# One product over all 64 keys instead of two over 32: window attention's weighted values on eight 64x32 tiles, with the probabilities copied between partition quarters by DMA

## The chip, the cores and the metric

The kernel runs on one core of one Trainium2 chip. The metric is the device time of one execution in microseconds, the median of several runs. The engines are named as in the profile: PE is TensorE (PEld its weight loads), DVE VectorE, ACT ScalarE, POOL GpSimd, and SP the engine that issues most DMAs.

## The reference

Input is x of 32 sequences x 256 tokens x 128 features, float32. Four residual blocks follow each other, each on the layer norm of its input:

```
x = x + window_attention(norm(x))      # block "P": 16 heads of 8, 2 key/value heads, window 32
x = x + butterfly_ffn(norm(x))         # block "F": 128 -> 512 -> gelu -> 128
x = x + linear_attention(norm(x))      # block "L": elu + 1, 16 heads of 8
x = x + butterfly_ffn(norm(x))         # block "G": the same weights as F
```

In the window attention a block of 32 queries looks at 64 keys (its own 32 and 16 on either side), masked to `(u >= t) & (u < t + 32)` for query t and key u. So each query sees exactly 32 of the 64 keys: of the keys u and u + 32 exactly one is allowed. The probabilities are a softmax over them, and the output is `einsum('bhntu,bhnud->bhntd', probs, vb)`.

## The kernel before, in words

The 8,192 tokens are worked on in 16 groups g of 512 tokens (TILES = 4 tiles j of 128 tokens, each with four windows of 32 queries). Each engine runs a list of steps, called a turn, over and over; a step with lag n in turn t works on group t - n, so several groups are in flight, one in each block. The order inside a turn and the lags are written out by hand in a function `turn` for each engine, and again in tables (PRODUCTS, VECTOR, PROBS, ...) from which the counts of the semaphore waits are made. COVERED lists waits of PE that another wait already implies. PE is in order: a product whose input or PSUM bank isn't ready holds all that are behind it. The first turns also carry the products that multiply out the butterfly weights (steps X.*).

The path of window attention for one tile j of a group is:

- `scores` (L491, W.S j): eight products on 64x32 tiles of the array, 512 columns each, write the scores of 64 keys for 16 heads into the two banks of `ps_s`. Their keys lie in `kx`, which `spread_keys` (L328) fills with eight DMAs from `kv_rows` in DRAM once the last scores of the previous group are done (there is one `kx`).
- DVE: `merge_halves` (L1018, W.cp) puts the allowed one of u and u + 32 in place, `row_max`, `subtract_max`, then `scores_transposed` (L1038, W.tr) transposes 32x32 blocks, so that keys lie on partitions.
- ACT: `probs_out` (L810, W.E) takes the exponential of 512 elements per partition into `probs_m`, one of 2 buffers.
- POOL: `probs_parted` (L419, W.um) multiplies the merged probabilities with two 0/1 masks (`keep`): one half for keys u < 32, one for u >= 32, 1,024 elements per partition into `probs_t`, one of 2 buffers.
- PE: `weighted_values` (L508, W.PV) makes 16 products on 32x32 tiles, 256 columns each. They use eight different tiles, twice: for part u = 0 and accumulated for u = 1.
- DVE: `head_outputs` (L1045 to L1052) transposes, and divides by the sum, which comes as a column of ones in the values `vx`.

The values come from `kv_rows` by `spread_values` (L340, eight DMAs for a group) into `vx_t`, and a DVE transpose into `vx`. A float32 product shows as two records in the trace.

Of the kernel before, what the change touches and what calls it, by code (L numbers as in the profile page):

```python
# [9 lines left out]
ALU = mybir.AluOpType  # L10
# [19 lines left out]
PARTS = SPAN // WIN  # L30
STAGES = HID.bit_length() - 1
INNER = P.bit_length() - 1
KVW = DIM + HEADS
FIRST = [("ident", P), ("last_half", WIN), ("keep", PARTS * WIN), ("wq", P), ("wkv", 2 * KV * HD), ("bq", 1), ("bkv", 1), ("inside", TSPAN), ("bo", P)]
# [33 lines left out]
]  # L68
PHI = [
    ("L.k1", 5), ("L.q", 4), ("L.k0", 4),  # L70
]
PROBS = [
    ("W.E3", 3), ("W.E0", 2), ("W.E1", 2), ("W.E2", 2),
]
POOL_STEPS = [
    ("L.rv", 6), ("L.nm", 6), ("L.rstd", 6), ("L.nmr", 6), ("P.rv", 0), ("P.nm", 0),
    ("P.rstd", 0), ("P.nmr", 0), ("F.rv", 4), ("F.nm", 4), ("F.rstd", 4), ("F.nmr", 4),
    ("W.rv", 3), ("W.nm", 3), ("W.rstd", 3), ("W.nmr", 3),
]
NORMED = [  # L80
    ("L.xn", 6), ("P.xn", 0), ("F.xn", 4), ("W.xn", 3),
# [5 lines left out]
    ("W.um2", 3), ("W.um3", 3), ("W.um0", 2), ("W.um1", 2),  # L87
]
TURNS = NG + 7
CHUNKS = {"a": [0, 1], "b": [2, 3]}  # L90
COVERED = {
    ("F.down", "F.up0"), ("F.down", "F.up2"), ("F.down", "F.up3"), ("F.down", "X.d6"), ("F.down", "bank"),
# [4 lines left out]
    ("G.up3", "X.wT"), ("L.k0", "L.xT"), ("L.k1", "L.xT"), ("L.kv", "L.k0"), ("L.kv", "bank"),  # L97
    ("L.oT", "L.out0"), ("L.out0", "L.q"), ("L.out1", "L.kv"), ("L.out1", "L.q"), ("L.out1", "bank"),
    ("L.q", "bank"), ("P.kv", "P.xT"), ("P.q", "P.xT"), ("W.PV0", "bank"), ("W.S1", "P.q"),
# [10 lines left out]
WINDOW = [[0, 1, 2, 3], [1, 0, 3, 2]]  # L110
# [31 lines left out]
def window_and_linear_attention_with_butterfly_ffn(  # L142
    nc, x, first_c, later_c, outer_c, vones_c, w_exp_t, w_con, up_m, down_m, out,
):
    with ExitStack() as ctx:
# [54 lines left out]
        vx = sb("vx", [P, TILES, KV, PARTS, 32])  # L200
# [3 lines left out]
        probs_m = sb("probs_m", [P, 2, KV, HPK, WIN])  # L204
        probs_t = sb("probs_t", [P, 2, PARTS, KV, HPK, WIN])
# [56 lines left out]
        kx_in = Count(sem("kx_in"), [("P.kx", 0)], 16 * HPK)  # L262
        v_in = Count(sem("v_in"), [("P.v", 0)], 16 * 4 * KV)
# [32 lines left out]
        def _(sp):  # L296
# [51 lines left out]
            def turn(t):  # L348
                for g in due(t, 2):
                    spread_keys(g)  # L350
                for g in due(t, 0):
                    load_x(g)
                for g in due(t, 2):
                    spread_values(g)
                for g in due(t, 7):
                    store_y(g)
                for g in due(t, 1):
                    store_keys(g)
# [7 lines left out]
        def _(pool):  # L366
# [58 lines left out]
            def turn(t):  # L425
                for g in due(t, 4):
                    add_bias(g, "W", bffn_s, "W.proj", "F.down")
                for g in due(t, 3):
                    probs_parted(g, 2)
                for g in due(t, 6):  # L430
                    normalise(g, "L")
                if t == 2:
                    ffn_bias()
                for g in due(t, 0):
                    normalise(g, "P")
                for g in due(t, 3):
                    probs_parted(g, 3)
# [6 lines left out]
                for g in due(t, 6):  # L444
                    add_bias(g, "L", bffn_s, "L.proj", "G.down")
                for g in due(t, 1):
                    add_bias(g, "P", bo_s, None, "W.proj")
                for g in due(t, 3):
                    normalise(g, "W")
# [8 lines left out]
        def _(pe):  # L458
# [38 lines left out]
            def weighted_values(g, j):  # L497
# [154 lines left out]
            def turn(t):  # L652
                for g in due(t, 2):
                    scores(g, 3)
                for g in due(t, 6):
                    ffn_up(g, "G", 3)
                for g in due(t, 5):
                    linear_out(g, 1)
                for g in due(t, 6):
                    ffn_up(g, "G", 0)  # L660
                    ffn_up(g, "G", 2)
                for g in due(t, 3):
                    heads_transposed(g)
                for g in due(t, 5):
                    linear_transposed(g)
                if t == 1:
                    up_stage(2, "b")
                for g in due(t, 6):
# [632 lines left out]
```

## Time and profile before

| what | value |
|---|---|
| three runs | 596.56, 597.85, 598.96 us; median 597.85 us |
| the profiled execution | 597.42 us, span 595.6 us |
| busy: PE, POOL, DVE, ACT | 553.9, 446.7, 445.7, 336.7 us |
| granted PE clock, mean | 0.986 |
| instructions | 16,572 |

The span is from the first to the last instruction of the profiled execution; its own time is 1.8 us longer. Busy times are of each engine by itself, and overlap.

### The profile page before, as it was taken

How to read it: one execution, taken by the hardware profiler on the slowest of the kernel's cores; microseconds unless marked ns; L12 is line 12 of the kernel's file. 1: busy time of each engine (PE TensorE's matmuls, PEld its weight loads, DVE VectorE, ACT ScalarE, POOL GpSimd, SP SyncE). 2: the span in 40 equal slices, each digit the busy share in tenths (PEclk: the TensorE clock that was granted, in tenths of full speed). 3: DMA queues.
4: the chain of work that ended last, by engine and by line, in shares of the span. 5: the costliest groups of instructions: out<-in, count | busy, mean ns of one | idle time of the engine just before them, and what ended most of it. 6: DMA issues, size and time to landing. Idle time of an engine off the chain costs nothing.

```text
span 595.6 us, 16572 instructions
## 1 busy us (share of the span) xinstructions
PE 553.9 (93%) x6068; PEld 355.3 (60%) x6068; DVE 445.7 (75%) x1270; ACT 336.7 (57%) x574; POOL 446.7 (75%) x645
## 2 busy tenths in 40 slices
PE   3867698989999999999999999999999999999986
PEld 2533354556756656666666675665666666777663
DVE  5498878898888878787887888787877878654430
ACT  1321355366667666665666566766666666766532
POOL 6064778798979878897979798887887795956530
PEclk9996989999999999999999999999999999999998
DMA  9410201010101020111101010101010100000001
GB/s 316 134 37 15 52 7 46 13 41 16 39 24 46 25 47 20 33 37 29 43 21 43 16 42 26 45 26 43 21 34 20 29 24 2 19 3 19 0 19 35
DMA packets 37904, 22.48 MB, mean 38 GB/s; under 512 B 8384, under 2 KB 35520, under 8 KB 37824
## 3 DMA queue, kind: packets, MB, share of 16 engines
q1 hardware_dynamic: 35376, 17.21, 11.1%
q10 hardware_dynamic: 2448, 4.22, 2.0%
q8 instruction: 48, 0.79, 0.6%
q14 instruction: 32, 0.26, 0.2%
HBM read 15.91 MB, written 5.51 MB: 36 GB/s over the span
## 4 chain that ended last, share of the span: by engine, by line
PE 82%; DVE 7%; issue 3%; POOL 2%; DMA 1%; ACTq 1%; SPq 1%; ACT 1%; DVEq 0%; POOLq 0%
PE ring L523 20%; PE ring L535 18%; PE ps_o L508 10%; PE ps_s L491 9%; PE ring L472 7%; PE ring L546 5%; PE ring L566 4%; PE ring L606 3%; PE ring L555 2%; PE ring L583 2%; PE ring L576 1%; DVE u_t L289 1%; SPq L328 1%; DMA x_P<-in_x 1%; PE ring L595 1%
## 5 line engine op out<-in xcount | busy, mean ns | idle before, releaser
L419 POOL TENSOR_TENSOR probs_t<-probs_m,first 128x1024 f32<-128x1024 f32 x64 | 150.4, 2362 | 34.7 <-ACT probs_m L810 26.3
L792 ACT ACT_TABLE_LOAD x60 | 77.0, 1283 | 10.8 <-issue 9.7
L802 ACT ACTIVATE hid_G<-ring,b 128x512 f32<-128x512 f32 x64 | 44.0, 687 | 62.0 <-PE ring L523 61.2
L491 PE MATMUL ps_s<-kx,q_t 64*32 64x512 f32 x1024 | 71.0, 611 | 6.8 <-DVE merged L1031 4.3
L508 PE MATMUL ps_o<-probs_t,vx 32*32 32x256 f32 x2048 | 72.5, 392 | 3.1 <-DVE vx L1113 2.8
L523 PE MATMUL ring<-xT_G,w1b 128*128 128x512 f32 x128 | 65.7, 619 | 1.7 <-DVE x_F L1003 1.0
L1018 DVE COPY_PREDICATED ps_s<-first,ps_s 128x512 f32<-128x512 uint32 x64 | 43.6, 682 | 28.0 <-PE ps_s L491 27.6
L535 PEld LDWEIGHTS ring<-w,hid_G 128*128 128x128 f32 x512 | 59.5, 192 | 3.5 <-ACT hid_G L802 1.7
L535 PE MATMUL ring<-w,hid_G 128*128 128x128 f32 x512 | 59.9, 275 | 1.8 <-DVE x_L L1003 1.0
L523 PE MATMUL ring<-xT_F,w1b 128*128 128x512 f32 x128 | 59.2, 605 | 0.7 <-ACT xT_F L780 0.7
L535 PE MATMUL ring<-w,hid_F 128*128 128x128 f32 x512 | 59.9, 275 | 0.0
L535 PEld LDWEIGHTS ring<-w,hid_F 128*128 128x128 f32 x512 | 58.6, 192 | 0.8 <-issue 0.8
L802 ACT ACTIVATE hid_F<-ring,b 128x512 f32<-128x512 f32 x64 | 43.9, 687 | 23.3 <-PE ring L523 23.2
L810 ACT ACTIVATE probs_m<-merged_t 128x512 f32<-128x512 f32 x64 | 39.4, 620 | 22.4 <-POOL probs_t L419 17.2
L1045 DVE STREAM_TRANSPOSE ps_o<-ps_o 128x512 f32<-128x512 f32 x64 | 45.5, 711 | 7.6 <-PE ps_o L508 7.3
L508 PEld LDWEIGHTS ps_o<-probs_t,vx 32*32 32x32 f32 x2048 | 31.5, 106 | 29.1 <-DVE mv_W L982 10.6
L1031 DVE TENSOR_TENSOR merged<-ps_s,rowmax 128x512 f32<-128x512 f32 x64 | 44.0, 687 | 2.8
L523 PEld LDWEIGHTS ring<-xT_F,w1b 128*128 128x128 f32 x128 | 23.0, 189 | 36.4 <-issue 34.5
L1038 DVE STREAM_TRANSPOSE merged_t<-merged 128x512 f32<-128x512 f32 x64 | 44.4, 695 | 0.2 <-ACT probs_m L810 0.2
L1025 DVE TENSOR_REDUCE rowmax<-ps_s 128x16 f32<-128x512 f32 x64 | 43.1, 674 | 0.9 <-issue 0.3
L523 PEld LDWEIGHTS ring<-xT_G,w1b 128*128 128x128 f32 x128 | 21.4, 194 | 22.3 <-issue 21.3
L566 PEld LDWEIGHTS ring<-later,xT_L 128*128 128x128 f32 x128 | 23.2, 189 | 14.7 <-issue 12.3
(114 smaller groups left out, 1071.5 us busy)
## 6 DMA issues: line engine op xcount, KB each, us to landing
kx<-kv_rows SPq DMA_DIRECT2D x128, 40.0 KB, 2.2
x_P<-in_x SPq DMA_DIRECT2D x16, 256.0 KB, 3.2
out_x<-x_G SPq DMA_DIRECT2D x16, 256.0 KB, 2.3
vx_t<-kv_rows SPq DMA_DIRECT2D x128, 8.0 KB
up_s<-in_up_m ACTq DMA_DIRECT2D x7, 256.0 KB, 7.0
down_s<-in_down_m ACTq DMA_DIRECT2D x7, 256.0 KB, 6.9
kv_rows<-kv_t SPq DMA_DIRECT2D x16, 80.0 KB, 1.6
later<-in_later_c SPq DMA_DIRECT2D x1, 584.0 KB, 4.1
```

The lines of the kernel that those rows point to most:

```text
L419: nc.gpsimd.tensor_tensor(probs_t[:, j % 2].rearrange("p u k h t -> p u (k h) t"), probs_m[:, j % 2].rearrange("p (a k) h t -> p a (k h) t ...
L491: last = nc.tensor.matmul(ps_s[32 * i:32 * i + 32, a], q_t[half, P * j + 32 * c:P * j + 32 * c + 32], kx[half, :, TSPAN * j + 32 * c:TSPAN ...
L508: last = nc.tensor.matmul(ps_o[32 * c:32 * c + 32, a, 0:HPK * WIN], vx[rows, j, a, u], probs_t[rows, j % 2, u, a], start=(u == 0), stop=(u ...
L523: nc.tensor.matmul(bank(name)[:], w1b[:, P * c:P * (c + 1)], x_t[s][:], start=True, stop=True).then_inc(product.sem, 1)
L535: last = nc.tensor.matmul(bank(name)[:, P * j:P * (j + 1)], hid[s][:, c, P * j:P * (j + 1)], w2[:, c], start=(c == 0), stop=(c == CH - 1))
L566: last = nc.tensor.matmul(bank(name)[:, 2 * P * i:2 * P * (i + 1)], x_t["L"][:, P * j:P * (j + 1)], wl_s[:, P:3 * P], start=True, stop=True)
L792: nc.scalar.activation(unused[:, i:i + 1], half[0:1, 0:1], function)
L802: nc.scalar.activation(hid[s][:, c], bank(name)[:], ACT.Gelu, bias=b1[:, c:c + 1]).then_inc(drained[BANK[name]].sem, 1)
L1018: nc.vector.copy_predicated(merged_s, last_half.bitcast(mybir.dt.uint32).rearrange("p (a t) -> p a t", a=1) .to_broadcast([P, HEADS, WIN]) ...
L1031: nc.vector.tensor_tensor(merged[:, j % 2].rearrange("p k h t -> p (k h) t"), halves()[0], m, ALU.subtract).then_inc(drained["S"].sem, 1)
L1038: nc.vector.transpose(merged_t[:, j % 2].rearrange("p k h t -> p (k h t)"), merged[:, j % 2].rearrange("p k h t -> p (k h t)")).then_inc(v ...
L1045: nc.vector.transpose(ps_o[:, :, 0:HPK * WIN], ps_o[:, :, 0:HPK * WIN]).then_inc(vec.sem, 1)
```

## The change

Weighted values become eight products for a tile, each over 64 partitions (all 64 keys of a window at once) instead of sixteen over 32. For this the keys u < 32 of a window and those u >= 32 must lie on neighbouring 32-partition quarters, and both quarters need the probabilities:

- ACT writes the exponential twice (1,024 elements per partition in one instruction, its input read twice), straight into `probs_t`, which has a buffer for each of the four tiles now; `probs_m` goes.
- `spread_probs`, new on SP: for each tile, four DMAs of 32 partitions x 2 KB copy each quarter's block into the neighbouring quarter, from `probs_t` to `probs_t`.
- POOL masks in place: 1,024 elements per partition, with one mask whose content depends on the quarter. It waits for the DMAs.
- `spread_values` takes other offsets, and WINDOW, which says which window lies in which quarter, changes for the second key/value head.
- The order of the turn and the lags of every engine are written anew, with the banks of the products, the waits that COVERED leaves out, and TURNS = NG + 9 for NG + 7.

```diff
+PAIR = 2
-        vx = sb("vx", [P, TILES, KV, PARTS, 32])
+        vx = sb("vx", [P, TILES, KV, PAIR, 32])
-        probs_m = sb("probs_m", [P, 2, KV, HPK, WIN])
-        probs_t = sb("probs_t", [P, 2, PARTS, KV, HPK, WIN])
+        probs_t = sb("probs_t", [P, TILES, PAIR, KV, HPK, WIN])
+        spread = [Count(sem(f"spread{j}"), [(f"W.d{j}", 0)], 16 * 4) for j in range(TILES)]
 # SP
-                        c = WINDOW[kv][i]
+                        c = WINDOW[kv][i & ~1] + i % PARTS
+            def spread_probs(g, j):
+                sp.wait_ge(probs.sem, probs.after(g, f"W.E{j}"))
+                for i in range(4):
+                    own, other = slice(32 * i, 32 * i + 32), slice(32 * (i ^ 1), 32 * (i ^ 1) + 32)
+                    sp.dma_start(probs_t[other, j, i % PAIR].rearrange("p k h t -> p (k h t)"),
+                                 probs_t[own, j, i % PAIR].rearrange("p k h t -> p (k h t)")
+                                 ).then_inc(spread[j].sem, 16)
 # SP's turn: spread_probs 3, load_x, store_keys, spread_values, spread_probs 0, store_y,
 #            spread_probs 1, spread_keys, spread_probs 2
 #    before: spread_keys, load_x, spread_values, store_y, store_keys
 # POOL, probs_parted
-                pool.wait_ge(product.sem, product.after(g if j >= 2 else g - 1, f"W.PV{(j - 2) % 4}"))
-                pool.wait_ge(probs.sem, probs.after(g, f"W.E{j}"))
+                pool.wait_ge(spread[j].sem, spread[j].after(g, f"W.d{j}"))
+                parts = probs_t[:, j].rearrange("p s k h t -> p (s k h) t")
                 nc.gpsimd.tensor_tensor(
-                    probs_t[:, j % 2].rearrange("p u k h t -> p u (k h) t"),
-                    probs_m[:, j % 2].rearrange("p (a k) h t -> p a (k h) t", a=1).to_broadcast([P, PARTS, HEADS, WIN]),
-                    keep.rearrange("p (u a t) -> p u a t", u=PARTS, a=1).to_broadcast([P, PARTS, HEADS, WIN]), ALU.mult
+                    parts, parts, keep.rearrange("p (a t) -> p a t", a=1).to_broadcast([P, PAIR * HEADS, WIN]), ALU.mult
                 ).then_inc(parted.sem, 1)
 # PE, weighted_values
-                for u in range(PARTS):
+                for s in range(PAIR):
                     for a in range(KV):
-                        for i in range(4):
-                            rows, c = slice(32 * i, 32 * i + 32), WINDOW[a][i]
-                            last = nc.tensor.matmul(ps_o[32 * c:32 * c + 32, a, 0:HPK * WIN], vx[rows, j, a, u],
-                                                    probs_t[rows, j % 2, u, a], start=(u == 0), stop=(u == PARTS - 1))
+                        for b in range(2):
+                            rows, c = slice(64 * b, 64 * b + 64), WINDOW[a][2 * b + s]
+                            last = nc.tensor.matmul(ps_o[32 * c:32 * c + 32, a, 0:HPK * WIN], vx[rows, j, a, s],
+                                                    probs_t[rows, j, s, a], start=True, stop=True)
 # PE's turn: G.up0, G.up1, W.oT, L.oT, G.up2, P.xT, W.proj, L.xT, L.proj, P.kv, W.PV0, W.S0, L.k0, L.k1, L.q,
 #    G.down, F.xT, W.PV1, W.S1, L.kv, F.up2, F.up0, F.up1, F.up3, W.PV2, W.S2, G.xT, L.out1, F.down,
 #    G.up3, W.S3, W.PV3, L.out0, P.q
 #    before: W.S3, G.up3, L.out1, G.up0, G.up2, W.oT, L.oT, G.up1, P.q, W.proj, L.xT, P.xT, L.proj, L.q,
 #    W.PV0, W.S0, L.k0, L.k1, G.down, F.xT, W.PV1, W.S1, F.up3, F.up0, F.up2, F.up1, P.kv, L.kv, W.PV2, W.S2,
 #    G.xT, L.out0, F.down, W.PV3
 # ACT, probs_out
-                act.wait_ge(parted.sem, parted.after(g if j >= 2 else g - 1, f"W.um{(j - 2) % 4}"))
+                act.wait_ge(product.sem, product.after(g - 1, f"W.PV{j}"))
                 act.wait_ge(vec.sem, vec.after(g, f"W.tr{j}"))
-                nc.scalar.activation(probs_m[:, j % 2].rearrange("p k h t -> p (k h t)"),
-                                     merged_t[:, j % 2].rearrange("p k h t -> p (k h t)"), ACT.Exp
-                                     ).then_inc(probs.sem, 1)
+                scores = merged_t[:, j % 2].rearrange("p (a k) h t -> p a (k h t)", a=1)
+                nc.scalar.activation(probs_t[:, j].rearrange("p s k h t -> p s (k h t)"),
+                                     scores.to_broadcast([P, PAIR, HEADS * WIN]), ACT.Exp).then_inc(probs.sem, 1)
```

The lines that begin with # in the diff are a summary of the orders of the turns, without the start-up steps.

## Rows read from the trace of the kernel before

**Rows 1.** The page: busy time by engine, and the chain that ended last by engine.

```profile
PE 553.9 (93%) x6068; PEld 355.3 (60%) x6068; DVE 445.7 (75%) x1270; ACT 336.7 (57%) x574; POOL 446.7 (75%) x645
...
PE 82%; DVE 7%; issue 3%; POOL 2%; DMA 1%; ACTq 1%; SPq 1%; ACT 1%; DVEq 0%; POOLq 0%
```

**Rows 2.** One turn as a stretch: busy us (x instructions) of each engine, clock, DMA share.

```profile
core 0: us, PE busy (x) PEld busy (x) DVE busy (x) ACT busy (x) POOL busy (x), PEclk, DMA share, GB/s
300.00:332.45 32.45, 32.45 (x380) 21.00 (x372) 26.53 (x78) 20.83 (x36) 27.77 (x41) 1.00 0.13 33
```

**Rows 3.** The chain of waits within that turn: start us, us, what.

```profile
305.78 1.02 PE ps_o L508 x32
306.80 1.02 PE ps_s L491 x16
...
308.87 0.49 PE ring L606 x4
309.37 1.72 PE ring L523 x4
...
312.81 0.86 PE ring L583 x2
313.67 0.89 PE ring L546 x8
314.56 0.87 PE ring L472 x8
```

**Rows 4.** One PV and one S, records by line: duration min/median/max, first and last start.

```profile
L508 PE MATMUL ps_o<-probs_t,vx x32: 374/374/398, 305.7 to 306.4; 32*32 32x256 f32 x32
...
L491 PE MATMUL ps_s<-kx,q_t x16: 589/601/613, 306.7 to 307.2; 64*32 64x512 f32 x16
```

**Rows 5.** Timeline of PE: the small products of P.kv before two different followers.

```profile
81.70 0.48 PE L576 MATMUL ring<-xT_P,first 128*32 128x160 f32 x8
82.11 1.09 PE L508 MATMUL ps_o<-probs_t,vx 32*32 32x256 f32 x32
...
107.65 0.48 PE L576 MATMUL ring<-xT_P,first 128*32 128x160 f32 x8
107.94 0.48 PE L595 MATMUL ring<-v_ext,phi_k 128*32 128x33 f32 x32
```

**Rows 6.** The L508 records by stretch.

```profile
0.00:120.00 120.00, 15.71 (x384) 6.44 (x384) 0.94 0.26 77
120.00:510.00 390.00, 52.43 (x1536) 23.15 (x1536) 1.00 0.12 30
510.00:530.00 20.00, 4.37 (x128) 1.93 (x128) 1.00 0.05 16
```

**Rows 7.** Groups by line of POOL and ACT: busy, mean ns, idle before.

```profile
L419 POOL TENSOR_TENSOR probs_t<-probs_m,first 128x1024 f32<-128x1024 f32 x64 | 150.4, 2362 | 34.7 <-ACT probs_m L810 26.3 <-PE ps_s L491 8.4
...
L810 ACT ACTIVATE probs_m<-merged_t 128x512 f32<-128x512 f32 x64 | 39.4, 620 | 22.4 <-POOL probs_t L419 17.2 <-DVE merged_t L1038 5.3
...
L818 ACT ACTIVATE phi_k<-neg_k 128x256 f32<-128x256 f32 x32 | 13.4, 418 | 1.0
```

**Rows 8.** Waits within the turn of Rows 2: us, times, longest.

```profile
POOL rv_F L378 <- DVE mv_F L982: 2.1, 1, 2.1
...
DVE x_W L1003 <- PE ring L546: 1.6, 1, 1.6
DVE ps_s L1018 <- PE ps_s L491: 1.3, 1, 1.3
...
POOL probs_t L419 <- ACT probs_m L810: 0.7, 1, 0.7
```

**Rows 9.** Timeline of SP's queue in the turn: start, us of issuing, line, count.

```profile
307.98 5.02 SPq L328 DMA_DIRECT2D kx<-kv_rows  x8
...
317.13 2.74 SPq L340 DMA_DIRECT2D vx_t<-kv_rows  x8
```

**Rows 10.** The key DMAs (L328), from issue to landing.

```profile
DMA to landing us min/median/max: 2.1/2.2/3.2
```

More of the change, by code:

```diff
@@ L348, in turn @@
             def turn(t):
-                for g in due(t, 2):
-                    spread_keys(g)
+                for g in due(t, 3):
+                    spread_probs(g, 3)
                 for g in due(t, 0):
                     load_x(g)
+                for g in due(t, 1):
+                    store_keys(g)
                 for g in due(t, 2):
                     spread_values(g)
+                    spread_probs(g, 0)
                 for g in due(t, 7):
                     store_y(g)
+                for g in due(t, 2):
+                    spread_probs(g, 1)
                 for g in due(t, 1):
-                    store_keys(g)
+                    spread_keys(g)
+                for g in due(t, 2):
+                    spread_probs(g, 2)
             for t in range(TURNS):
@@ L652, in turn @@
             def turn(t):
+                for g in due(t, 8):
+                    ffn_up(g, "G", 0)
+                if t == 5:
+                    down_stage(6)
+                for g in due(t, 8):
+                    ffn_up(g, "G", 1)
+                if t == 4:
+                    up_stage(5, "a")
+                for g in due(t, 5):
+                    heads_transposed(g)
+                for g in due(t, 7):
+                    linear_transposed(g)
+                for g in due(t, 8):
+                    ffn_up(g, "G", 2)
@@ L653, in turn @@
                 for g in due(t, 2):
-                    scores(g, 3)
+                    norm_transposed(g, "P", "P")
+                for g in due(t, 5):
+                    project(g, "W", o_wt, wo_s)
                 for g in due(t, 6):
-                    ffn_up(g, "G", 3)
-                for g in due(t, 5):
-                    linear_out(g, 1)
[L659 to L663, printed above, removed]
@@ new lines, in turn @@
+                if t == 3:
+                    up_stage(3, "a")
+                for g in due(t, 2):
+                    attention_kv(g)
+                if t == 4:
+                    up_stage(4, "b")
+                for g in due(t, 4):
+                    weighted_values(g, 0)
+                for g in due(t, 3):
+                    scores(g, 0)
+                for g in due(t, 6):
+                    linear_kv_rows(g, 0)
+                if t == 5:
+                    up_transposed()
@@ new lines, in turn @@
+                for g in due(t, 6):
+                    linear_kv_rows(g, 1)
+                if t == 4:
+                    up_stage(6, "a")
+                if t == 3:
+                    down_stage(1)
+                for g in due(t, 6):
+                    linear_q(g)
+                if t == 4:
+                    up_stage(5, "b")
+                    down_stage(4)
+                for g in due(t, 8):
+                    ffn_down(g, "G")
+                for g in due(t, 5):
+                    norm_transposed(g, "F", "W")
@@ new lines, in turn @@
+                if t == 3:
+                    up_stage(3, "b")
+                for g in due(t, 4):
+                    weighted_values(g, 1)
+                if t == 2:
+                    up_stage(0, "b")
+                for g in due(t, 3):
+                    scores(g, 1)
+                if t == 2:
+                    up_stage(1, "b")
+                for g in due(t, 6):
+                    linear_state(g)
+                if t == 3:
+                    down_stage(2)
+                if t == 2:
+                    up_stage(1, "a")
@@ new lines, in turn @@
+                if t == 3:
+                    up_stage(4, "a")
+                for g in due(t, 5):
+                    ffn_up(g, "F", 2)
+                    ffn_up(g, "F", 0)
+                    ffn_up(g, "F", 1)
+                if t == 2:
+                    up_stage(2, "a")
+                for g in due(t, 5):
+                    ffn_up(g, "F", 3)
+                for g in due(t, 4):
+                    weighted_values(g, 2)
+                if t == 2:
+                    up_stage(2, "b")
@@ L688, in turn @@
+                for g in due(t, 3):
+                    scores(g, 2)
+                for g in due(t, 7):
+                    norm_transposed(g, "G", "L")
+                if t == 3:
+                    down_stage(3)
+                if t == 4:
+                    down_stage(5)
+                for g in due(t, 6):
+                    linear_out(g, 1)
+                if t == 4:
+                    up_stage(6, "b")
                 if t == 0:
@@ L736, in turn @@
-                for g in due(t, 2):
-                    weighted_values(g, 2)
-                if t == 0:
-                    up_stage(1, "b")
-                for g in due(t, 1):
-                    scores(g, 2)
-                for g in due(t, 5):
-                    norm_transposed(g, "G", "L")
-                if t == 1:
-                    up_stage(5, "a")
-                for g in due(t, 4):
+                    ffn_down(g, "F")
+                for g in due(t, 7):
+                    ffn_up(g, "G", 3)
@@ L906, in turn @@
-                for g in due(t, 2):
-                    probs_out(g, 0)
-                    probs_out(g, 1)
-                if t == 3:
-                    down_stage_out(6)
-                for g in due(t, 6):
-                    gelu(g, "G", 3)
-                    gelu(g, "G", 0)
+                for g in due(t, 9):
+                    gelu(g, "G", 0)
+                    gelu(g, "G", 1)
+                for g in due(t, 6):
+                    copy_out(g, "W.oT", o_wt[:], "W.proj")
+                if t == 4:
+                    down_stage_out(0)
@@ L914, in turn @@
+                for g in due(t, 8):
+                    copy_out(g, "L.oT", o_lt[:], "L.proj")
+                for g in due(t, 9):
                     gelu(g, "G", 2)
                 for g in due(t, 3):
-                    copy_out(g, "W.oT", o_wt[:], "W.proj")
-                for g in due(t, 5):
-                    copy_out(g, "L.oT", o_lt[:], "L.proj")
-                if t == 2:
+                    keys_input_out(g)
+                if t == 4:
+                    up_stage_out(3, "a")
+                    down_stage_out(1)
@@ new lines, in turn @@
+                for g in due(t, 7):
+                    copy_out(g, "L.xT", x_t["L"][:], "L.q", "L.k0", "L.k1")
+                if t == 5:
+                    up_stage_out(5, "a")
+                for g in due(t, 5):
+                    probs_out(g, 2)
+                if t == 0:
+                    up_stage_out(0, "a")
+                for g in due(t, 5):
+                    probs_out(g, 3)
+                for g in due(t, 7):
+                    linear_k_parts(g, 0)
+                if t == 6:
+                    down_stage_out(6)
@@ new lines, in turn @@
+                for g in due(t, 7):
+                    linear_k_parts(g, 1)
+                    linear_q_parts(g)
+                if t == 3:
+                    up_stage_out(0, "b")
+                if t == 5:
+                    up_stage_out(4, "b")
+                if t == 3:
+                    up_stage_out(1, "b")
+                    up_stage_out(1, "a")
+                if t == 4:
+                    up_stage_out(3, "b")
+                if t == 5:
+                    up_stage_out(5, "b")
@@ new lines, in turn @@
+                if t == 6:
+                    up_weights_out()
+                for g in due(t, 6):
+                    copy_out(g, "F.xT", x_t["F"][:], *UPS["F"])
+                if t == 3:
+                    up_stage_out(2, "b")
+                for g in due(t, 4):
+                    probs_out(g, 0)
+                if t == 4:
+                    up_stage_out(4, "a")
+                if t == 5:
+                    down_stage_out(4)
+                for g in due(t, 6):
+                    gelu(g, "F", 2)
@@ L920, in turn @@
+                if t == 5:
+                    up_stage_out(6, "b")
+                for g in due(t, 6):
+                    gelu(g, "F", 0)
+                if t == 3:
+                    up_stage_out(2, "a")
+                for g in due(t, 6):
+                    gelu(g, "F", 1)
+                if t == 4:
                     down_stage_out(2)
                 for g in due(t, 6):
-                    gelu(g, "G", 1)
-                if t == 1:
-                    up_stage_out(2, "a")
-                if t == 2:
+                    gelu(g, "F", 3)
@@ L926, in turn @@
+                for g in due(t, 4):
+                    probs_out(g, 1)
+                if t == 5:
+                    up_stage_out(6, "a")
+                for g in due(t, 8):
+                    copy_out(g, "G.xT", x_t["G"][:], *UPS["G"])
+                    gelu(g, "G", 3)
+                if t == 5:
+                    down_stage_out(5)
+                if t == 4:
                     down_stage_out(3)
-                for g in due(t, 1):
+                for g in due(t, 3):
                     attention_q_out(g)
-                if t == 3:
-                    up_weights_out()
@@ L1133, in turn @@
             def turn(t):
-                for g in due(t, 0):
-                    moments(g, "P")
+                if t == 4:
+                    up_outer_stage(1)
+                for g in due(t, 6):
+                    moments(g, "L")
+                for g in due(t, 5):
+                    phi_k_made(g, 0)
+                for g in due(t, 2):
+                    row_max(g, 0)
+                    subtract_max(g, 0)
+                for g in due(t, 5):
+                    phi_k_made(g, 1)
+                for g in due(t, 2):
+                    scores_transposed(g, 0)
+                for g in due(t, 5):
+                    phi_q_made(g)
                 for g in due(t, 7):
                     residual(g, "G", "G.down", "L")
-                for g in due(t, 2):
-                    merge_halves(g, 1)
                 for g in due(t, 3):
@@ L1142, in turn @@
                 for g in due(t, 2):
[L1143 to L1147 removed]
+                    merge_halves(g, 1)
                 for g in due(t, 5):
@@ L1150, in turn @@
                 for g in due(t, 2):
-                    scores_transposed(g, 0)
+                    row_max(g, 1)
+                    subtract_max(g, 1)
+                for g in due(t, 0):
+                    moments(g, "P")
+                for g in due(t, 2):
+                    scores_transposed(g, 1)
+                    merge_halves(g, 2)
                 for g in due(t, 3):
@@ L1179, in turn @@
                     row_max(g, 3)
-                if t == 2:
-                    up_outer_stage(1)
-                for g in due(t, 2):
+                    scores_transposed(g, 2)
                     subtract_max(g, 3)
@@ L1185, in turn @@
                     residual(g, "W", "W.proj", "P")
+                for g in due(t, 2):
+                    scores_transposed(g, 3)
+                for g in due(t, 3):
                     moments(g, "W")
-                for g in due(t, 2):
-                    scores_transposed(g, 2)
+                if t == 0:
+                    down_outer_stage(0)
+                for g in due(t, 0):
+                    attention_kv_out(g)
                 for g in due(t, 5):
@@ L1255, in constants @@
     last_half = (t < row).astype(np.float32)
-    keep = np.concatenate([row >= t, row < t], axis=1).astype(np.float32)
+    keep = np.where(np.arange(P)[:, None] // WIN % PARTS == 0, row >= t, row < t).astype(np.float32)
     vones = np.zeros((P, KV * SPAN), np.float32)
```

215 lines of the change are left out of this document (36 added, 179 removed), and 56 rows, old and new, of tables (COVERED, PRODUCTS, VECTOR).

## The prediction

> **What bounds the kernel now.** I read the page first. PE is busy 93% of the span, no other engine above 75%, and 82% of the chain that ended last is PE [rows 1]. A busy share is a mean over start, middle and end, so I then cut out one turn from the middle: 32.45 us long, PE busy for all of it at the full clock, DVE 26.53 us, ACT 20.83 us, POOL 27.77 us [rows 2]. The chain of waits in that turn is made of PE pieces alone, each beginning where the one before ends [rows 3]. So in the middle of the kernel PE's stream of products is the period, and a turn shortens by what leaves PE, until the next engine's own work is reached.
>
> How near is that? POOL waited in this turn 2.1 us for F's moments and 0.7 us for probabilities [rows 8]; 32.45 - 2.8 = 29.65 us is what its stream needs if it never waits. DVE waited at least 1.6 + 1.3 us for PE, so it needs at most 29.5 us [rows 2, 8]. PE can give up about 2.8 us a turn before another engine sets the period.
>
> **What a PV costs.** W.PV takes 1.02 us before the scores start, and W.S also takes 1.02 us [rows 3]. PV has 32 records of 256 columns, S has 16 of 512, on eight different tiles each. At 2.4 GHz (clock 1.00, [rows 2]) L583's 2 records of 512 columns take 0.86 us [rows 3]: 0.43 us a record, 0.84 ns a column, hence 0.215 us for 256 columns. If nothing overlapped, PV would take 32 x 0.215 = 6.9 us. It takes 1.02, and its records start over 0.7 us [rows 4]: four batches of eight, 0.215 us apart (3 x 0.215 = 0.65). S starts over 0.5 us: two batches 0.43 us apart. So eight tiles run side by side in both, 4 x 0.215 = 0.86 and 2 x 0.43 = 0.86, and 0.16 us is left in each. What that rest is: P.kv takes 0.41 us when followed by a PV, whose tiles have another shape, and 0.29 us when followed by L.kv with tiles of the same shape [rows 5]. A change of tile shape costs 0.12 us of the 0.16.
>
> **The change on PE.** After it, PV has 16 records of 256 columns on eight tiles: two batches, 0.43 us, and a rest of 0.04 us. It now has the tile shape of S (64x32), and stands next to S in all four pairs, so the 0.12 us between the two goes: a pair takes 1.02 + 0.47 = 1.49 us for 2.04, a saving of 0.55 us, 2.20 us for four. Before, P.kv and L.kv were neighbours and now aren't: +0.12 us. The other products are the same in number and shape. Sum: -2.08 us, a turn of 30.37 us. Bounds: if the change of shape costs nothing once it is gone, 4 x 0.43 - 0.12 = 1.6 us; at the other end 4 x 0.55 = 2.2 us.
>
> The nearest row for eight products of 64 rows is S itself, same tiles, same two banks, so I take its full overlap. A doubt: the two row groups now write into one bank at the same time. But four row groups did so in PV before, and that overlapped eightfold [rows 4]. The Trainium skill has a rule against it (TensorEngine Tiling (Array Packing), Restrictions and Gotchas, Gotcha 1): different row tiles cannot access the same PSUM bank simultaneously. By that rule the old PV would have taken 3.4 us (32 x 0.215 over two banks), and the trace has 1.02; by it the new one would gain nothing, which is a rival below.
>
> **The change elsewhere.** ACT: 256 elements take 418 ns and 512 take 620 [rows 7], so 1,024 take about 1,030 ns: +0.41 us, 1.6 us a turn, to 22.4 us busy of 30.4. It lies beside PE; by the lists, exponential and GELU alternate as often in a turn as before, so no table load is added. POOL: the same 1,024 elements, 2.36 us [rows 7], one mask operand as before; I take no change, bounds 0 and +0.1 us each. DVE: nothing is added.
>
> SP: a value DMA takes 2.74 / 8 = 0.34 us to issue, a key DMA 5.02 / 8 = 0.63 us [rows 9]. Both bound a probability DMA; with its 32 rows it is nearest the value DMA (8 x 4 rows). 16 x 0.34 = 5.5 us a turn (10.0 at most), beside 7.8 us for keys and values: SP is occupied for less than 20 of 30 us. What matters is lateness. From the end of W.E to the mask there are now 4 x 0.34 + 2.2 us to landing [rows 10] = 3.6 us, 5.7 at most, against nothing before. From W.S j of a group to its W.PV j PE's new list has a whole turn, 28 us. I laid the new lists side by side with the durations of before, PE end to end, each other engine in order behind what it needs. The masks then start 5 us or more after the landing for all four tiles, and finish from 1.6 us (j = 2) to 9 us (j = 1) before their PV. No step of PE waits; the nearest are S2 and F.up3, 0.8 us behind what DVE makes.
>
> Behind spread_probs on SP wait the keys: kx is free when S3 ends, and must be filled before S0. Issue 5.02 + landing 2.2 = 7.2 us [rows 9, 10]. PE's new list has between S3 and S0: PV3 0.47, L.out0 0.49, P.q 0.86, G.up0, 1, 2 2.58, W.oT and L.oT 0.87, W.proj and L.proj 1.8, P.xT and L.xT 0.87, P.kv 0.41, PV0 0.35 = 8.7 us [rows 3, 5]. Cover 1.5 us. The spread_probs ahead of it in the queue (j = 1) waits for W.E1, which my layout ends 4.7 us before S3 does, so it is done issuing 3 us before the keys are due.
>
> Tightest is POOL: 29.65 us of work in 30.37, and DVE's 29.5 at most. In my layout POOL is left 1.1 us of waiting (for W's moments). Two engines so near to PE's period, in lists that wait on each other, will cost PE a little; I put 0.2 us a turn on it (between 0 and the next rival's 0.9).
>
> **The sum.** Of 2,048 PV records 384 lie before 120 us [rows 6], where groups 0 to 2 fill the pipeline and PE has holes (mean clock 0.94 there, 1.00 later). The other 13 groups run where PE is full. Their saving: 12 turns x (2.08 - 0.2) = 22.6 us; the last group's PVs stand without an S behind, 4 x 0.43 = 1.7 us. The first three groups: between 0 and 3 x 2.08 = 6.2; their turns are set by chains through DVE and ACT, and the 3.6 us of copy lies in these too, I take 2. Start and end are otherwise rewritten with about as many turns from P.xT to G.down of a group (by the lists, a little over six before and after): I take 0, bounds +-5 us. Together 26.3 us off the profiled 597.42: 571. The median of the runs is 0.4 us above the profiled one, which is below what matters: 571.5.
>
> **The rivals.**
> - POOL or DVE becomes the bound. Price: a period of 31.3 us instead of 30.6 (POOL's 29.65 and waits of 1.6 us, a little over half of its present ones). 12 x 1.15 + 1.7 + 1 = 16.5 us: 581. For it: 29.65 is just under 30.4. Against: the lists leave POOL only two short waits.
> - The products don't overlap eightfold: two row groups on one bank take turns, a PV then takes 2 x 2 x 0.215 + 0.16 = 1.02 us as before. The gain is nothing but shape changes, 0.36 us a turn, under 5 us, and the new order may lose as much: 597. Against it: old PV and S. The rule of the Trainium skill cited above (TensorEngine Tiling (Array Packing), Gotcha 1) would give this result.
> - Slower: the DMA chain holds PE. The place is SP's queue: if W.E1 is late by more than the 3 us, its four DMAs push spread_keys back, S0 waits, and with it all DVE work that makes the next W.E1. It costs nothing until 3 + 1.5 us are used up; it decides once the stall passes 32.45 - 30.57 = 1.9 us a turn, so at a copy or exponential 6.4 us later than I have it. At 3 us a turn beyond the cover the turn is 33.6 us, 12 x 1.1 = 13 us more than before, less the 3.7 us saved outside: 607. For it: ACT must change tables between the GELUs and this exponential, and in-order queues pass delays on. Against: 6.4 us is a lot.
>
> **How the numbers follow.** The forecast (PE sets the period, 565 to 577) 0.68; POOL or DVE 0.19, 576 to 590; no overlap 0.07, 590 to 600; slower 0.06, 600 to 620. A range from 563 to 588 leaves out the last two, a little of the second and the tail of the first: about 2 in 10. Half a per cent, 3 us, is about what can be told from no change here. Faster: 0.68 + 0.19 + 0.02 of the third = 0.89, less 0.01 for a start that goes wrong: 0.88. Within: 0.05. Slower: 0.07.
>
> **What the new profile would show.** PV's group at L508's place with 1,024 records, a PV of 0.43 to 0.47 us from its start to S's; a middle turn of 30.4 to 30.6 us with PE at least 49.5 of 50 us busy; exponentials of about 1,030 ns; masks of 2.36 us. Wrong would be: new waits of PE for the keys' DMA or of POOL for the copies; POOL's busy share near 95% and PE's below; PV at 0.86 us or more between its start and the next product; or a filling phase that takes back several us.

## The result, and the profile after

The changed kernel takes 569.99 us (median of 4 runs, 569.17 to 573.61) beside 597.2 us of the kernel before on the same chip (596.21 to 598.96): a ratio of 0.956, with a 95% interval from 0.953 to 0.958. That is 27.2 us less, 4.6% by the medians and 4.4% by the ratio. The forecast was 571.5 us, from 563 to 588.

The page of the profiled execution (span 568.3 us, its own time 570.1), busy time and the chain that ended last, against [rows 1]:

```profile
PE 520.6 (92%) x5044; PEld 343.1 (60%) x5044; DVE 443.2 (78%) x1270; ACT 353.8 (62%) x570; POOL 447.9 (79%) x645
...
PE 72%; DVE 2%; POOL 2%; issue 1%; ACT 0%; DVEq 0%; ACTq 0%; POOLq 0%
```

PE lost 33.3 us of busy time and 1,024 records; DVE and POOL moved by 2.5 us or less, ACT gained 17.1. The span fell by 27.3 us, 6.0 less than PE's busy time did, because PE stands still for longer, 4.3 of the 6.0 us before P.q of group 4, while the pipeline fills. The next view gives busy time by stretch:

```profile
50.00:100.00 50.00, 35.34 (x376) 18.68 (x356) 44.39 (x108) 19.75 (x30) 33.13 (x42) 0.86 0.25 58
...
300.00:350.00 50.00, 50.00 (x526) 33.41 (x532) 44.52 (x130) 37.90 (x62) 45.86 (x68) 1.00 0.29 70
```

In the middle PE is full (50.00 of 50 us, clock 1.00). One turn of it, cut to its new length, answers to [rows 2]:

```profile
300.00:330.19 30.19, 30.19 (x310) 20.11 (x309) 26.56 (x78) 21.96 (x36) 27.81 (x41) 1.00 0.28 70
```

The turn is 30.19 us for 32.45, and 2.26 us are what PE lost. DVE's 26.56 and POOL's 27.81 us of busy time are those of before; ACT's grew from 20.83 to 21.96: four exponentials of 1.04 us for four of 0.62, and four table loads (1.28 us each) where the turn before had five. The DMA share went from 0.13 to 0.28. The chain of waits in that turn, against [rows 3], is again PE alone; and beside it PE's timeline of the same pair:

```profile
304.96 0.41 PE ring L592 x8
305.37 0.59 PE ps_o L524 x16
305.96 0.86 PE ps_s L507 x16
306.82 1.92 PE ring L582 x8
```

```profile
305.30 0.66 PE L524 MATMUL ps_o<-probs_t,vx 64*32 64x256 f32 x16
305.75 1.06 PE L507 MATMUL ps_s<-kx,q_t 64*32 64x512 f32 x16
306.75 1.99 PE L582 MATMUL ring<-later,xT_L 128*128 128x256 f32 x8
```

(In the views of matrix products `x8` counts records, and the second number is the time to the end of the last one.) By the start times a PV holds PE for 0.45 us and the S behind it for 1.00: 1.45 us for the pair, where two times 1.02 stood before. The chain view divides the same 1.45 us otherwise (0.59 and 0.86), because it counts the ends of records; the sum is what to read.

What was near to waiting, from the waits of the same turn, and SP's queue in it, against [rows 8] and [rows 9]:

```profile
POOL rv_W L396 <- DVE mv_W L1008: 0.7, 1, 0.7
```

```profile
299.57 2.52 SPq L330 DMA_DIRECT2D kx<-kv_rows  x4
307.25 5.71 SPq L350 DMA_DIRECT2D probs_t<-probs_t  x8
...
314.27 2.72 SPq L342 DMA_DIRECT2D vx_t<-kv_rows  x8
317.03 2.43 SPq L350 DMA_DIRECT2D probs_t<-probs_t  x4
...
322.35 2.41 SPq L350 DMA_DIRECT2D probs_t<-probs_t  x4
327.22 3.78 SPq L330 DMA_DIRECT2D kx<-kv_rows  x6
```

POOL waits 0.7 us in the turn, for W's moments, and for no copy. Four copies take 2.4 us to issue, 0.6 each. (Counts of 4 and 6 for the key DMAs are groups cut by the window; a group has eight of them.) The page's groups of POOL's masks and ACT's exponentials, against [rows 7]:

```profile
L437 POOL TENSOR_TENSOR probs_t<-probs_t,first 128x1024 f32<-128x1024 f32 x64 | 151.4, 2367 | 7.5 <-DMA probs_t<-probs_t 7.5
...
L829 ACT ACTIVATE probs_t<-merged_t 128x1024 f32<-128x1024 f32 x64 | 65.6, 1045 | 7.9 <-DVE merged_t L1064 7.8
```

All of POOL's waits for copies come to 7.5 us in the whole run: three waits, for masks that start at 46.5, 50.6 and 63.3 us, none in the middle.

**Where the 27.3 us of span came from.** The product P.q (L583 before, L599 after) marks the turns. Of group 4 it begins at 119.98 us before and 118.60 after: 1.4 us gained while the pipeline fills. From there to P.q of group 15 it is 354.95 us before (to 474.93) and 330.17 after (to 448.77): 24.8 us gained in 11 turns, 2.25 each in the mean and 2.26 in the steady ones. What follows takes 120.67 and 119.53 us: 1.1 us. Together 27.3. P.q stands elsewhere in the new list, so the three parts are not cut at exactly the same work.

### The profile page after: what moved, and what is told of

The parts are those of the page before. It is cut to its first block, busy times and chain, and to the rows that moved or that the text cites. A ratio compares the mean times of both kernels' runs of the same rounds, so it can differ in the third digit from the quotient of the medians.

```text
span 568.3 us, 14681 instructions
## 1 busy us (share of the span) xinstructions
PE 520.6 (92%) x5044; PEld 343.1 (60%) x5044; DVE 443.2 (78%) x1270; ACT 353.8 (62%) x570; POOL 447.9 (79%) x645
## 4 chain that ended last, share of the span: by engine, by line
PE 72%; DVE 2%; POOL 2%; issue 1%; ACT 0%; DVEq 0%; ACTq 0%; POOLq 0%
PE ring L551 18%; PE ring L539 17%; PE ps_s L507 7%; PE ring L488 7%; PE ps_o L524 5%; PE ring L582 5%; PE ring L562 4%; PE ring L622 3%; PE ring L571 2%; PE ring L599 2%; PE ring L611 1%; PE ring L592 1%; POOL xn_L L408 0%; POOL probs_t L437 0%; DVE stats_F L1003 0%
## 5 line engine op out<-in xcount | busy, mean ns | idle before, releaser
L437 POOL TENSOR_TENSOR probs_t<-probs_t,first 128x1024 f32<-128x1024 f32 x64 | 151.4, 2367 | 7.5 <-DMA probs_t<-probs_t 7.5
L829 ACT ACTIVATE probs_t<-merged_t 128x1024 f32<-128x1024 f32 x64 | 65.6, 1045 | 7.9 <-DVE merged_t L1064 7.8
L539 PE MATMUL ring<-xT_G,w1b 128*128 128x512 f32 x128 | 64.2, 607 | 0.7 <-ACT xT_G L798 0.7
L524 PE MATMUL ps_o<-probs_t,vx 64*32 64x256 f32 x1024 | 43.1, 393 | 0.9 <-DVE o_w L1078 0.9
L862 ACT ACTIVATE q_t<-ring,first 128x512 f32<-128x512 f32 x16 | 11.0, 688 | 46.3 <-PE ring L599 46.3
L507 PEld LDWEIGHTS ps_s<-kx,q_t 64*32 64x32 f32 x1024 | 16.9, 107 | 27.0 <-DVE merged L1057 11.4
L582 PE MATMUL ring<-later,xT_L 128*128 128x256 f32 x128 | 31.9, 392 | 0.0
```

Source lines behind the costliest of these rows:

```text
L437: nc.gpsimd.tensor_tensor(parts, parts, keep.rearrange("p (a t) -> p a t", a=1).to_broadcast([P, PAIR * HEADS, WIN]), ALU.mult).then_inc(p ...
L507: last = nc.tensor.matmul(ps_s[32 * i:32 * i + 32, a], q_t[half, P * j + 32 * c:P * j + 32 * c + 32], kx[half, :, TSPAN * j + 32 * c:TSPAN ...
L539: nc.tensor.matmul(bank(name)[:], w1b[:, P * c:P * (c + 1)], x_t[s][:], start=True, stop=True).then_inc(product.sem, 1)
L582: last = nc.tensor.matmul(bank(name)[:, 2 * P * i:2 * P * (i + 1)], x_t["L"][:, P * j:P * (j + 1)], wl_s[:, P:3 * P], start=True, stop=True)
L829: nc.scalar.activation(probs_t[:, j].rearrange("p s k h t -> p s (k h t)"), scores.to_broadcast([P, PAIR, HEADS * WIN]), ACT.Exp).then_inc ...
```

## The experiments

**e1: the old products in the new kernel.** The order, the copies and the masks of the change stay; 0.01 is added to the mask (not shown in the cut).

```diff
                 for s in range(PAIR):
                     for a in range(KV):
-                        for b in range(2):
-                            rows, c = slice(64 * b, 64 * b + 64), WINDOW[a][2 * b + s]
+                        for i in range(4):
+                            rows, c = slice(32 * i, 32 * i + 32), [[0, 1, 2, 3], [1, 0, 3, 2]][a][i]
                             last = nc.tensor.matmul(ps_o[32 * c:32 * c + 32, a, 0:HPK * WIN], vx[rows, j, a, s],
-                                                    probs_t[rows, j, s, a], start=True, stop=True)
+                                                    probs_t[rows, j, s, a], start=(s == 0), stop=(s == PAIR - 1))
```

> The changed kernel with the old form of the products: sixteen on 32x32 tiles, two accumulated, in the new order with the copies and masks of the new one. The quarters hold other keys than this form needs, so it sums over mixed windows, and 0.01 is added to the mask so that no sum is zero; its time is what is asked. Theory (the whole gain is in PE's stream at these products): a PV goes back to 1.02 us with a change of tile shape before S, a middle turn from 30.19 to about 32.55 us, the time from 570 to about 597 us. Rival (the newly written order of the turns gave the gain or a good part of it, and fuller cover would take up longer products): a turn under 32 us and less than 590 us.

Measured: 599.08 us beside 597.15 of the kernel before, a ratio of 1.005 (1.002 to 1.008), so the gain is gone. The profiled execution was the slowest of its ten (605.54 us), with a longer fill; the turn is read from its middle. From PE's timeline (start, us, records):

```profile
309.30 1.09 PE L524 MATMUL ps_o<-probs_t,vx 32*32 32x256 f32 x32
310.32 1.09 PE L507 MATMUL ps_s<-kx,q_t 64*32 64x512 f32 x16
...
341.85 1.09 PE L524 MATMUL ps_o<-probs_t,vx 32*32 32x256 f32 x32
```

The PV is at 1.02 us again, and the next turn's same PV stands 32.55 us later, as the theory had it. The new order with its copies is worth nothing by itself: it costs 0.1 us a turn, which fits the 0.12 us that [rows 5] gives for P.kv and L.kv no longer side by side.

**e2: as many records as before, but in the new tile shape.** The loop `for s in range(PAIR)` became `for s in [0, 1, 0, 1]`.

> The changed kernel with each of the eight products made twice in a row of batches, same tiles, the second overwriting the first: as many records and columns as the old form has (32 x 256), but with the 64x32 tile shape that S has. Theory (batches of eight cost 0.215 us each, and a change of shape costs 0.12 to 0.15 us by itself): PV 0.455 + 0.43 = 0.89 us, a turn of 31.9 us, about 592 us, which is some 0.6 us a turn less than the old tiles in the same kernel. Rival (columns alone count, the shape is free once the pipeline is full): the same time as the old tiles.

Measured: 592.87 us, ratio 0.994 (0.992 to 0.995).

```profile
305.20 1.09 PE L507 MATMUL ps_s<-kx,q_t 64*32 64x512 f32 x16
...
315.15 1.09 PE L524 MATMUL ps_o<-probs_t,vx 64*32 64x256 f32 x32
316.03 1.07 PE L507 MATMUL ps_s<-kx,q_t 64*32 64x512 f32 x16
...
337.12 1.09 PE L507 MATMUL ps_s<-kx,q_t 64*32 64x512 f32 x16
```

A PV of 0.88 us, and a turn of 337.12 - 305.20 = 31.92 us. So the two parts of the gain come apart: from the old tiles (32.55) to the same number of columns in S's shape (31.92) is 0.63 us a turn, 0.16 for each of four pairs; from there to half of them (30.19) is 1.73 us, 0.43 for each PV. The whole rest of 0.16 us of an old PV was the change of shape. The rival is out. By the medians it is 6.2 of the 29.1 us between e1 and the changed kernel. One difference beside the shape remains: e1 accumulates its second set of products and e2 overwrites. No run separates the two; that accumulating costs nothing is only argued, from [rows 4], where the four batches of an old PV, two of them accumulating, start within 0.7 us, as 3 x 0.215 us asks for columns alone.

**e3: one bank for each row group.** In the output, `ps_o[32 * c:32 * c + 32, a, ...]` became `ps_o[32 * c:32 * c + 32, b, ...]`.

> The changed kernel with the output bank of a product chosen by its row group (b) instead of by the key/value head (a), so that the two row groups never write one bank; the heads of half the windows land in the other head's place. Theory (two row groups in one bank overlap fully as long as they write different quarters of it): PV stays at 0.455 us, the turn at 30.19, 570 us. Rival (sharing a bank costs part of the overlap): PV shorter than 0.45 us, down to 0.3, a turn up to 0.6 us shorter, 562 to 566 us.

Measured: 572.12 us beside 597.15, ratio 0.956 (0.952 to 0.960), as the changed kernel.

```profile
333.11 0.66 PE L524 MATMUL ps_o<-probs_t,vx 64*32 64x256 f32 x16
333.57 1.06 PE L507 MATMUL ps_s<-kx,q_t 64*32 64x512 f32 x16
```

The PV still takes 0.46 us and the turn 30.19 us. Two row groups that write different quarters of one bank lose nothing against two that write different banks. Two row groups that write the same quarter of a bank at the same time weren't tried.

**e4: each copy made twice.** The semaphore counts eight copies a tile, and `spare` is a new buffer (both not shown in the cut).

```diff
                                  probs_t[own, j, i % PAIR].rearrange("p k h t -> p (k h t)")
                                  ).then_inc(spread[j].sem, 16)
+                    sp.dma_start(spare[other, j], probs_t[own, j, i % PAIR].rearrange("p k h t -> p (k h t)")
+                                 ).then_inc(spread[j].sem, 16)
```

> The changed kernel with sixteen more copies a turn: each copy is made a second time into a spare buffer, on the same semaphore, so that the masks wait for both. Issuing a copy took 0.59 us in the changed kernel's trace, where the prediction had 0.34 us. Theory (SP's queue is a serial resource that is busy some 19 us of a turn at 0.59 us a copy; twice the copies fill it): SP needs 32 x 0.59 for copies, 5.0 for keys, 2.7 for values and 1.6 for the rest, 28.3 us, plus what it waits, and from the exponential of tile 2 to the keys it is a closed chain, so the turn rises to between 30.5 and 32 us, and PE waits for the keys: 574 to 592 us. Rival (the prediction's 0.34 us holds as the cost, the median is only a wait inside the queue): 19 us of a turn, nothing moves, 570 us.

Measured: 619.09 us (2 runs) beside 597.13, ratio 1.037 (1.034 to 1.041): 49 us slower than the changed kernel. The theory's direction is right and its size too small. SP's queue, and two waits of a window of 100 us (250 to 350):

```profile
308.65 0.59 SPq L354 DMA_DIRECT2D spare<-probs_t  x1
309.28 0.59 SPq L351 DMA_DIRECT2D probs_t<-probs_t  x1
309.92 0.59 SPq L354 DMA_DIRECT2D spare<-probs_t  x1
...
334.67 0.58 SPq L331 DMA_DIRECT2D kx<-kv_rows  x1
```

```profile
DVE stats_P L1006 <- DMA x_P<-in_x: 8.3, 2, 5.1
...
PE ps_s L510 <- DMA kx<-kv_rows: 2.6, 1, 2.6
```

Most copies begin 0.63 us apart without a gap, and they did at half as many a turn (2.4 us for four), so 0.6 us is the cost of issuing and not a wait that grows with the queue's load. From P.q of group 5 to that of group 15 (160.90 to 496.74 us) the turn is 33.6 us in the mean. SP's own work is 32 x 0.63 + 5.0 + 2.7 + 1.8 = 29.7 us of it. By the waits shown, the rest arises as x is loaded late behind sixteen copies, DVE waits up to 5.1 us for it, and the exponentials that follow from DVE's work let SP wait in turn (its queue is empty from 304.2 to 308.0 us, between the keys and the next copies). The middle is not all of the loss: of 48.4 us more of span, 11.2 lie before P.q of group 4, 36.8 in the 11 turns behind it and 0.4 after them; the expectation counted none for the fill. It is the mechanism of the third rival (SP's queue closes a chain), by another transfer than the one that it named.

**e5: no copies.** The masks wait for the exponentials.

> The changed kernel without the sixteen copies of a turn: the masks wait for the exponentials alone and each product sees its own quarter's probabilities in place of the neighbour's (a stale or doubled half, so the values are wrong). Theory (the copies are covered everywhere but in the first turns): the middle turn stays at 30.19 us, PE full, and the time falls by 0 to 3 us, to 567 to 570. Rival (copies take SBUF or queue time from the others, or the waits of POOL for them set part of the fill): a shorter middle turn, or more than 4 us gained before 120 us.

Measured: 570.0 us (566.67 to 572.2), ratio 0.953 (0.949 to 0.957): the same as the changed kernel. PE in the middle:

```profile
311.74 0.66 PE L524 MATMUL ps_o<-probs_t,vx 64*32 64x256 f32 x16
...
341.93 0.66 PE L524 MATMUL ps_o<-probs_t,vx 64*32 64x256 f32 x16
```

The turn is 30.19 us. P.q of group 4 begins at 115.89 us in this profile and at 118.60 in the changed kernel's, but the runs of either kernel scatter by 4 us or more. Another profile says how much of the 2.7 us is the copies: e3 has all of them and comes to the same P.q at 116.27 us, 0.4 us behind e5. So the copies cost little in the fill too, and the most of the 2.7 us is the difference between one execution and another.

**e6: one mask more a turn on POOL.** A multiply into a spare buffer ahead of the mask of tile 0.

> The changed kernel with one more mask multiply a turn on POOL (tile 0, into a spare buffer, 2.37 us). POOL waits 0.7 us of the 30.19 us in a middle turn, so its stream needs 29.5 us. Theory (POOL is the next bound, 0.7 us below PE): the turn becomes 29.5 + 2.4 = 31.8 us or somewhat more, 1.65 us above, 590 us with 12 to 13 such turns, and PE gets holes. Rival (some of POOL's stretches between instructions are slack that a fuller queue would close): a turn under 31 us, below 581 us.

Measured: 591.44 us (2 runs), ratio 0.991 (0.987 to 0.994). The turn is 31.77 us (P.q at 312.21 and 343.98), PE waits for POOL, and POOL is busy for 94.8 us of 100:

```profile
300.00:400.00 100.00, 95.92 (x965) 62.08 (x963) 84.31 (x247) 70.04 (x112) 94.81 (x127) 1.00 0.27 66
```

```profile
PE ring L493 <- POOL xn_F L409: 4.1, 3, 1.4
```

**e7: PE made lighter.** Both second feed-forward products run over two of four chunks (`for c in range(CH)` became `for c in [2, 3]`), which leaves those chunks' part out of the output.

> The changed kernel with the second products of both feed-forward blocks over two of their four chunks: PE loses 2 x 1.78 = 3.6 us a turn, to 26.6 us of work; the outputs lack those chunks. Theory (the other engines' streams are just below PE's): the turn falls by only 0.7 us to POOL's 29.5 us, or stops higher for the waits between lists that were ordered for PE, 29.5 to 30.2 us; 560 to 568 us, with PE holes in every turn. Rival (PE is the only bound for several us): a turn of 27 to 28 us, below 545 us.

Measured: 554.63 us (2 runs), ratio 0.929 (0.926 to 0.932). The middle turn is 29.45 us (P.q at 265.03 and 294.47). The chain of waits in the stretch from 300 to 331 us is mostly POOL's (the view breaks the line off):

```profile
by line: POOL probs_t L437 37.5%; issue 8.8%; POOL xn_F L408 6.0%; POOL xn_L L408 4.7%; POOL xn_P L408 4.7%; POOL xn_W L408 4.5%; POOL xb_L L424 4.0%; POOL xb_W L424 4.0%; POOL xb_F L424 4.0%; POOL xb_P L424 3.4%; POOL rstd_W L400 3.3%; POO
```

3.6 us less of PE work shortened the turn by only 0.74 us. The total fell by 15.4 us, more than I expected (560 to 568 us). By the starts of P.q the spans differ by 8.3 us in the 11 turns of the middle and by 7.6 us behind P.q of group 15, where POOL is busy for only 74 of 120 us and a lighter PE pays more; the fill gave nothing (119.44 us to P.q of group 4 for 118.60). POOL is the next bound in the middle alone. e6 and e7 agree on POOL's stream: 29.45 us, and 31.77 with a mask of 2.36 us more.

**e8: a hole in the fill.** DVE's `up_outer_stage(1)` moved from the start of turn 4 to turn 3, ahead of the residual of W.

> The changed kernel with the second outer stage of the up weights moved in DVE's list from the start of turn 4 to turn 3, behind subtract_max of tile 3. In the changed kernel's trace PE waits 5.4 us for it at 75.8 us, the longest hole of the fill. Theory (the hole is DVE's order): the product X.wT comes 3 to 4 us earlier, of which the residual that is pushed back takes some; the time falls by 1 to 3 us, 567 to 569 us. Rival (DVE is full there, and what goes first pushes the rest): within 1 us of the changed kernel.

Measured: 566.89 us (565.58 to 570.11), ratio 0.949 (0.946 to 0.952), with a profiled span of 568.3 us, the same as the changed kernel's. In that profile the hole only moved:

```profile
73.66 0.48 PE L592 MATMUL ring<-xT_P,first 128*32 128x160 f32 x8 [2.13 <-DVE x_W L1029]
...
76.31 1.11 PE L664 MATMUL ring<-first,u_t 128*128 128x128 f32 x4
79.48 1.11 PE L488 MATMUL ring<-first,xn_W 128*128 128x128 f32 x4 [2.05 <-POOL xn_W L408]
```

X.wT (L664) begins at 76.31 us for 75.79: in place of the wait of 5.4 us stand a longer one for W's head outputs before it (2.37 us) and the two that are shown, for W's residual, which was pushed back, and for W's norm. P.q of group 4 comes at 120.26 us, 1.7 later than in the changed kernel, and the part behind P.q of group 15 is 1.7 shorter (clock 1.00 behind 550 us for 0.90). But the profile is of the slowest of four runs. The median is 3.1 us below the changed kernel's, as the theory had it, the intervals of the two ratios do not overlap (0.946 to 0.952, and 0.953 to 0.958), and the three faster runs have a mean clock of 0.988 where the changed kernel's four have 0.976 to 0.979. So a small gain is likely; that it comes from the hole is not shown, since no profile of a faster run was kept.

## Why the prediction was right

The mechanism held: PE's stream sets the period, and a turn shortens by what leaves it. That the time came within 1.5 us (571.5 for 569.99) is in part luck, since several terms were off and cancel. Step by step:

- **PE's stream sets the period.** Shown from both sides: e1 gives back the whole gain by the products alone, and in the changed kernel PE has no hole in the middle; e6 and e7 show where POOL takes over.
- **Eight tiles side by side, 0.215 us a batch.** A PV is 0.45 us (forecast 0.43 to 0.47). The doubt over two row groups in one bank was unfounded (e3). The rule of the Trainium skill (TensorEngine Tiling (Array Packing), Restrictions and Gotchas, Gotcha 1) that different row tiles can't access the same PSUM bank simultaneously isn't what these runs show for different quarters of the bank; the measurement decides.
- **The change of tile shape** was mis-sized a little: 0.12 us from [rows 5], 0.16 us by e2. A pair saves 0.59 us, not 0.55. With 0.12 us for the parted P.kv the turn's sum is 4 x 0.59 - 0.12 = 2.24 us; forecast 2.08, measured 2.26, which is above the 2.2 us that the prediction gave as the upper end.
- **The 0.2 us a turn for small stalls** was wrong: there is none. The layout by hand of the new lists was a better guide than the caution put on top of it; it even had the right wait (POOL, for W's moments, 1.1 us; measured 0.7).
- **SP** was the term sized worst: a copy costs 0.6 us to issue, not 0.34. The nearest row was not the value DMA, with the same 32 rows, but the key DMA, the upper bound. A tile's copies take 2.4 + 2.0 us (the page's median from issue to landing), not 3.6. It did not matter, since the layout had 5 us or more of cover; e5 shows that the copies are free in the middle, and e4 that they no longer are when their number doubles.
- **POOL near the bound.** Forecast 29.65 us, shown 29.45. The first rival (POOL or DVE) lost by 0.74 us a turn: POOL is the next bound, not this one.
- **Fill and end**: forecast 2 + 1.7 us, found 1.4 and 1.1. The prediction counted 12 full turns at 1.88 us, 22.6; there are 11 between P.q of group 4 and of group 15, and they gave 24.8. With 2.26 us a turn its own sum would have been 12 x 2.26 + 3.7 = 30.8 us, 3.5 more than was found: a saving a turn that was too small was set off by a last turn that was counted as full and by a fill and an end that gave less.

The other two rivals, no overlap and a chain through SP, did not happen; e3 excludes the bank as a cause of loss, and e4 shows that a chain through SP exists, by the load of x and not by the keys alone, and has its price further on.

## What to carry to other kernels

Where an in-order engine is full, cost a change by the start-to-start distance of its products and by what stands next to them: here 0.63 of the 2.36 us between e1's turn and the changed kernel's, about a quarter, came from two products with the same tile shape being neighbours. Before trusting a saving, add up each other engine's stream without its waits, since it tells how much of the saving can be had (here 2.26 us were, and 0.74 more would be). A transfer that is hidden still takes issue time on its queue, and with 0.6 us each sixteen more of them a turn (e4) cost 3.4 us a turn.

## What the runs showed of the hardware

- A change of tile shape (32x32 to 64x32) costs 0.16 us (e2 against e1, which also differ in accumulating), all that a PV of before took over its columns; from 128x32 to 32x32 it costs 0.12 us [rows 5].
- Two row groups writing different quarters of one PSUM bank overlap fully: PV 0.45 us with a bank shared, 0.46 with a bank for each (e3).
- A 32-partition copy of 64 KB within SBUF takes 0.6 us of SP to issue and 2.0 us to land; a value DMA (8 x 4 rows, 8 KB) takes 0.34 us to issue, a key DMA of 40 KB 0.63.
- In the fill of the changed kernel the granted clock was 0.86 between 50 and 100 us, where PE was busy for 35.3 of 50 us and stood still for up to 5.4 us at a time; before the change it was 0.93 in the same stretch, with 41.3 us busy. Behind the hole of 5.4 us the four products on `xn_W` (L488) take 1.06 us, and in the middle 0.60 us: the lower and the upper level of the clock, 1.2 and 2.4 GHz.

```profile
75.79 1.11 PE L664 MATMUL ring<-first,u_t 128*128 128x128 f32 x4 [5.40 <-DVE u_t L291]
76.70 1.06 PE L488 MATMUL ring<-first,xn_W 128*128 128x128 f32 x4
...
313.01 0.60 PE L488 MATMUL ring<-first,xn_W 128*128 128x128 f32 x4
```
